# One Wg product per quad of graphs in the second pass, the attention mask added on TensorE, and the first quad's low parts moved to VectorE

## The reference, cut to what matters

```python
h = relu(layernorm(x))
# layer 0
D = abs(h[:, :, None, :] - h[:, None, :, :])      # 64 x 128 x 128 x 128
s = einsum('bijc,oc->bijo', D, W1) + b1           # 64 outputs
s = leaky(batchnorm(s, over=(b, i, j)))
s = einsum('bijo,uo->biju', s, W2)[..., 0] + b2
s = where(adj > 0, s, -9e15)
A = softmax(s, axis=-1)
y = einsum('bij,bjc->bic', A, h) @ Wg.T + bg
y = leaky(batchnorm(y, over=(b, i)))
x = x + concatenate([h, y], 2) @ Wt.T + bt
# layer 1: an attention of the usual kind with a mask, softmax over axis 1, elu, and x added
```

## Time and profile before

| | before |
|---|---|
| median of 3 runs | 1128.88 us |
| their range | 1128.56 to 1129.87 us |
| the profiled execution | 1126.25 us |
| its span | 1124.3 us |
| busy: PE, DVE, ACT, POOL | 1049.5, 1033.1, 1001.0, 567.6 us |
| PE matmul with W1 (line 789) | 1792, 422.8 us |
| PE `att_sum` (lines 931 and 932) | 128 + 128, 24.9 + 24.7 us |
| PE nodes with Wg (line 877) | 128, 18.8 us |

### The profile page before, as it was taken

How to read it: one execution, slowest core, us unless ns; L and a number is a source line. 1 busy time by engine, 2 the same in 40 slices (tenths; PEclk the granted TensorE clock), 3 DMA queues, 4 the chain that set the end, 5 groups by cost and what they waited for, 6 DMA issues and landing times.

```text
span 1124.3 us, 17526 instructions
## 1 busy us (share of the span) xinstructions
PE 1049.5 (93%) x6390; PEld 461.6 (41%) x6390; DVE 1033.1 (92%) x1381; ACT 1001.0 (89%) x1268; POOL 567.6 (50%) x331
## 2 busy tenths in 40 slices
PE   3899999999999899999999989999999999978997
PEld 1333333333333333333333444233333333357786
DVE  5899999999999999999999985899999999948897
ACT  3889898999999899999999978999999999934897
POOL 5687678778777877777787700111121122201430
PEclk9999999999999999999999999999999999989999
DMA  6345443454444344454444487999999999960012
GB/s 183 139 153 196 159 175 153 168 198 168 194 171 179 140 186 180 168 196 169 185 182 178 179 327 269 337 361 329 334 347 326 342 332 329 324 175 14 20 58 76
DMA packets 99060, 233.31 MB, mean 208 GB/s; under 512 B 9120, under 2 KB 46464, under 8 KB 98976
## 3 DMA queue, kind: packets, MB, share of 16 engines
q1 hardware_dynamic: 86704, 219.97, 53.5%
q0 software_dynamic: 2240, 7.34, 1.8%
q10 hardware_dynamic: 10032, 4.89, 1.7%
HBM read 124.43 MB, written 107.74 MB: 206 GB/s over the span
## 4 chain that ended last, share of the span: by engine, by line
PE 50%; DVE 23%; ACT 14%; issue 9%; POOL 3%; ACTq 1%; DMA 0%; DVEq 0%; POOLq 0%
PE psum L789 21%; PE psum L799 10%; ACT store L674 8%; DVE store L294 8%; PE psum L803 8%; DVE plain_st L1099 3%; PE psum L902 3%; ACT store L593 2%; POOL store L294 1%; PE psum L779 1%; PE psum L761 1%; DVE store L1131 1%; PE psum L877 1%; ACTq L678 1%; DVE bst L1283 1%
## 5 line engine op out<-in xcount | busy, mean ns | idle before, releaser
L294 POOL TENSOR_TENSOR store<-h_ext 128x2048 f32<-128x2048 f32 (+1 forms) x96 | 386.3, 4025 | 95.7 <-PE psum L789 95.7
L789 PE MATMUL psum<-store,w1tt_sb 128*64 128x512 f32 x1792 | 422.8, 598 | 10.9 <-ACT store L593 10.8
L294 DVE TENSOR_TENSOR store<-psum,h_ext 128x2048 f32<-128x2048 f32 x160 | 363.9, 2274 | 0.6 <-ACT h_ext L563 0.6
L593 ACT ACTIVATE store<-store 128x2048 f32<-128x2048 f32 x160 | 305.7, 1928 | 19.3 <-DVE store L294 11.8
L674 ACT ACTIVATE store<-store,st 128x1024 f32<-128x1024 f32 x192 | 227.9, 1240 | 0.0
L789 PEld LDWEIGHTS psum<-store,w1tt_sb 128*64 128x64 f32 x1792 | 122.6, 136 | 249.5 <-issue 214.4
L799 PE MATMUL psum<-store,w_twice 128*64 128x512 f32 x768 | 201.6, 602 | 5.4 <-DVE store L294 2.9
L294 DVE TENSOR_TENSOR store<-h_ext 128x2048 f32<-128x2048 f32 x64 | 146.1, 2283 | 16.3 <-PE psum L789 16.0
L1099 DVE BATCH_NORM_STATS2 plain_st<-store 128x6 f32<-128x512 f32 x256 | 160.5, 678 | 0.0
L803 PE MATMUL psum<-early 128*64 128x512 bf16 x1152 | 159.0, 382 | 0.0
L605 ACT COPY store<-psum 128x1024 f32<-128x1024 f32 x128 | 128.4, 1024 | 16.7 <-PE psum L789 11.6
(11 more groups left out here) (161 smaller groups left out, 1088.4 us busy)
## 6 DMA issues: line engine op xcount, KB each, us to landing
kept_products<-store SPq DMA_DIRECT2D x192, 512.0 KB, 2.9
store<-kept_products SPq DMA_DIRECT2D x192, 512.0 KB, 5.8
early<-score_skew POOLq DMA_DIRECT2D x14, 384.0 KB, 6.8
early<-adj SPq DMA_DIRECT2D x16, 256.0 KB, 3.5
early<-adj_t SPq DMA_DIRECT2D x16, 256.0 KB, 3.6
store<-x ACTq DMA_DIRECT2D x16, 256.0 KB, 5.3
out<-early SPq DMA_DIRECT2D x16, 256.0 KB, 2.3
score_skew<-early POOLq DMA_DIRECT2D x14, 128.0 KB, 6.1
```

The costliest lines, as they stand in the source:

```text
L294: return engine.tensor_tensor(t[:, :, 0:steps, :], nodes.unsqueeze(2).broadcast_to([C, 2, steps, N]), windows(h_ext[:, 2 * c, :], STEP * m ...
L593: nc.scalar.activation(t, t, ACT.Abs).then_inc(abs_ready, 1)
L789: last = nc.tensor.matmul(t[MID * g:MID * g + MID, b, :], w1tt_sb[:, 0:MID], diff[slot][:, g, b * BANK:b * BANK + BANK], start=True, stop= ...
```

## The change

1. `mix_at` takes a step: PE makes one quad's product with Wg at n = 14 + 16·k, ACT copies it at n = 17 + 16·k, for k = 0 to 13. All these use bank 4; `at_zero` now waits only for as many as were made before, `at_one` only for the two early ones.
2. `att_sum`: the mask comes first, as one bfloat16 matmul of 512 columns (`neg_ident`, -9e15 on the diagonal, times `none`, 1 where there is no edge); then four float32 matmuls give the transposed half. The plain half is added by DVE when it reads the bank (`att_scores`).
3. POOL makes `neg_ident` once and `none` for each quad (two buffers), ahead of `store_skew(j)`.
4. `s_half` is now read by DVE too, so the next load of it waits for `s_masked` in place of `s_sum`.
5. The first quad's low part is made by DVE at n = 1, not by POOL ahead of its loop.

```diff
+        none = sb("none", [128, 2, BANK], BF16)
+        neg_ident = sb("neg_ident", [128, 128], BF16)
...
         EARLY_MIX = 2
+        WEIGHED, WEIGHED_OUT = 14, 17
 
         def nodes_bank(u):
-            return psum[:, 4 + u % 2, :].rearrange("p (b n) -> p b n", b=QUAD)
-
-        def mix_at(n):
-            u, r = divmod(2 * n, 3)
-            return EARLY_MIX + u if r < 2 and 0 <= u < NQ - EARLY_MIX else None
+            return psum[:, 4 + (u == 1), :].rearrange("p (b n) -> p b n", b=QUAD)
+
+        def mix_at(n, step):
+            u, r = divmod(n - step, QCH)
+            return EARLY_MIX + u if r == 0 and 0 <= u < NQ - EARLY_MIX else None
+
+        def weighed_before(n):
+            return min(EARLY_MIX + so_far(WEIGHED, n), NQ)
...
-            low(0)
             for n in range(CHUNKS):
...
             def load_half(j):
                 pool.wait_ge(skew_stored[j % 2], 16 * (j // 2 + 1))
                 if j > 0:
-                    pool.wait_ge(s_sum, j)
+                    pool.wait_ge(s_masked, j)
...
+            def none_of(j):
+                if j >= 2:
+                    pool.wait_ge(s_sum, j - 1)
+                nc.gpsimd.tensor_scalar(none[:, j % 2, :].rearrange("p (b n) -> p b n", b=QUAD), no_edge[0][:, quad(j), :],
+                                        1.0, None, ALU.mult).then_inc(none_set, 1)
...
+            nc.gpsimd.tensor_scalar(neg_ident[:, :], ident[:, :], NEG, None, ALU.mult).then_inc(neg_set, 1)
             for j in range(NQ):
+                none_of(j)
                 if j < BY_POOL:
                     store_skew(j)
                     load_half(j)
...
-                if u < 2:
+                if u < EARLY_MIX:
                     pe.wait_ge(kept_ready, NKEPT)
                 else:
-                    pe.wait_ge(weighted_ready, u - 1)
+                    at_zero(QCH * (u - EARLY_MIX) + WEIGHED)
...
             def at_zero(n):
 
-                pe.wait_ge(weighted_ready, NQ)
+                pe.wait_ge(weighted_ready, weighed_before(n))
...
             def att_sum(j):
                 pe.wait_ge(half_summed, j + 1)
+                pe.wait_ge(none_set, j + 1)
+                if j == 0:
+                    pe.wait_ge(neg_set, 1)
                 at_zero(QCH * j + SUM)
-                for b in range(QUAD):
-                    nc.tensor.matmul(att[0][:, b, :], ident[:, :], s_half[:, b, 0:N], start=True, stop=False)
-                    last = nc.tensor.matmul(att[0][:, b, :], s_half[:, b, 0:N], ident[:, :], start=False, stop=True)
+                nc.tensor.matmul(att[0], neg_ident[:, :], none[:, j % 2, :], start=True, stop=False)
+                for b in range(QUAD):
+                    last = nc.tensor.matmul(att[0][:, b, :], s_half[:, b, 0:N], ident[:, :], start=False, stop=(b == QUAD - 1))
                 last.then_inc(s_sum, 1)
...
+                if n == 1:
+                    dve.wait_ge(y_mid, 1)
+                    nc.vector.tensor_tensor(y_part(0, 2), by_couple(y_rest[:, :]), y_part(0, 1), ALU.subtract).then_inc(y_split, 1)
...
-                nc.vector.scalar_tensor_tensor(s_shift[:, :, :], no_edge[0][:, quad(j), :], NEG, att[0], ALU.mult, ALU.add)\
+                nc.vector.tensor_tensor(s_shift[:, :, :], att[0], s_half[:, :, 0:N], ALU.add)\
                   .then_inc(s_masked, 1)
```

More of the change, by code:

```diff
@@ L216, in two_layers @@
         x_out, x_folded = sem("x_out"), sem("x_folded")
+        none_set, neg_set = sem("none_set"), sem("neg_set")
         weighted, weighted_ready, y_out = sem("weighted"), sem("weighted_ready"), sem("y_out")
@@ L698, in _ @@
                         load_x(q)
-                if mix_at(n) is not None:
-                    nodes_out(mix_at(n))
+                if mix_at(n, WEIGHED_OUT) is not None:
+                    nodes_out(mix_at(n, WEIGHED_OUT))
                 for step, do in ((Y, y_to_nodes), (EXP, exps)):
@@ L952, in _ @@
                     products_again(n + LEAD_PROD)
-                if mix_at(n) is not None:
-                    weighted_nodes(mix_at(n))
+                if mix_at(n, WEIGHED) is not None:
+                    weighted_nodes(mix_at(n, WEIGHED))
                 m = n - LAG_SCORE
```

4 lines of the change are left out of this document (2 added, 2 removed).

## The result

| | before | after |
|---|---|---|
| median (range) of 4 runs each | 1129.08 us (1128.56 to 1129.87) | 1119.90 us (1118.75 to 1121.02) |
| profiled execution, its span | 1126.25, 1124.3 us | 1118.91, 1116.9 us |
| busy: PE, DVE, ACT, POOL | 1049.5, 1033.1, 1001.0, 567.6 us | 1041.3, 1040.9, 1000.1, 609.1 us |

The account below looks back on a forecast made before the run. PE bounds pass 2's start, a DVE-ACT ring its rounds (20.32 us each). Terms -11.0 + 5.5 - 1.4 - 1.0 = -7.9 take the profiled 1126.25 to 1118.3, or 1121.0 us for the median; range 1114 to 1126.

Parts of the forecast that it names:

- Products out of the start: Start of pass 2: without the products with Wg, ACT runs at 1.12 us a chunk, gaining 11.0 us (bounds 8 to 11.7).
- the 0.7 taken off for PE's clock: Start of pass 2: gain cut from 11.7 to 11.0 us, as PE may stay at 1.2 GHz longer.
- The copy in the ring: Pass 2 rounds: ACT's copy between exponential and result costs 0.46 us in twelve rounds, 5.5 lost (bounds 0 to 11).
- the ring: Pass 2 rounds: DVE waits for ACT (0.43 us) and ACT for DVE (1.16), closing 20.32 us a round without PE.
- rival A: Pass 2 rounds: the chain through PE's scores and `att_sum` binds; 1.4 us gained instead of 5.5 lost, 1114.1; chance 0.12.
- `att_sum`, -1.4 at the end: Quads 14 and 15: PE's `att_sum` is 0.7 us shorter each, gaining 1.4 us (bounds 0 and 1.4); nothing in the rounds.
- The sum on DVE and the added waits: Pass 2: DVE's sum replaces the mask there at 0.68 us; waits for `none_set`, bank 4 and `s_masked` are covered; 0.
- POOL's masks: Pass 2 rounds: 16 masks of some 1.51 us on mostly idle POOL don't hold up DVE; cost 0.
- rival C: Pass 2 rounds: POOL's masks block DVE in the ring, costing 23 us, 1144; chance 0.08.
- Start of pass 1: PE begins 1.2 us later, but its 2.54 us wait for ACT goes; gain 1.0 (bounds: loss 1.3, gain 1.4).
- The caution about PE's slow pace: Start of pass 1: gain taken as 1.0 us, not 1.3, since PE's slow first us may last as long by the clock.

Follow-up runs that it names:

- Spread alone: Kernel before with only the products with Wg moved to one per quad (n = 14 + 16k, ACT's copy at n = 17 + 16k): median 1122.9 us, ratio 0.9956.
- copy outside: Changed kernel with products with Wg at n = 10 + 16k and ACT's copy at n = 12 + 16k, ahead of the exponential: median 1118.7 us, ratio 0.9912.
- all together: Changed kernel with ACT's copy ahead of the exponential, POOL's masks moved, loads of x on SP, products of no use on PE: 1118.8 us, ratio 0.9905.

## Why the prediction was right

It gave 1121.0 us, in a range of 1114 to 1126; 1119.9 came. By its own steps:

1. *Products out of the start, -11.0: -9.4.* ACT's rate held but for 0.01 (1.13 us a chunk for 1.12, some 0.4 in all), and the loads kept up (DMA at 1.01 to 1.10). Mis-sized was the 0.7 taken off for PE's clock and the wait before the exponential: the new waits for L805 are 1.27 us, and 0.83 stands before exponential 0 in place of the 0.21 that was carried over. With PE kept at 2.4 GHz the start came to 54.05 and 53.56.
2. *The copy in the ring, +5.5: +5.7 of the +6.94.* Spread alone, 20.80; copy outside, 20.32. The choice of the ring over the chain's reading (rival A, 1114.1) was the step that mattered most, and it rests on two waits, 0.43 and 1.16. The prediction has both "in every round"; ACT's is, but DVE's is missing in three rounds of before (at 779.64, 921.92 and 942.25), of which under 6. After the change the chain of waits itself shows the ring.
3. *`att_sum`, -1.4 at the end: about right.* It takes 1.20 us (895.89 to 897.09), DVE's wait for it in quad 15 (0.89 in the earlier trace rows) is gone, and ACT's wait before each of the two last exponentials falls from 4.37 or 4.38 to 3.62: 1.5 us in all. The other 1.5 us of the -3.02 was not foreseen. ACT's issues of the loads of x start when PE's last product made again is done, 0.70 behind the start of exponential 13 before (989.08) and 0.04 after (984.02); its last activation comes 1.16 sooner behind that exponential, and the second eight issues take 5.34 in place of 5.68. Of those sixteen issues the prediction said nothing, though they cost the changed kernel some 6 us (medians 1119.9 and 1113.8) and stood in the trace of before.
4. and 5. *The sum on DVE and the added waits, 0.* L1247 takes 0.68; no wait for bank 4, `none_set` or `s_masked` shows in the rounds.
6. *POOL's masks, 0: +1.2 us.* This step failed, in the direction of rival C and at a twentieth of its price. The row it rested on, a subtraction of 2.27 beside a mask of 1.51, was read as no contention; it shows no more than that this DVE instruction went free. Others didn't: in the changed kernel L1150 takes 1.52 to 1.79 in place of 1.23 where it meets POOL, L298 up to 2.80 in place of 2.27, and the masks of layer 0 that DVE holds up 2.46 to 4.23 in place of 1.49. The trace of before had a warning that the prediction didn't show:

```profile
919.60 1.64 DVE L1131 TENSOR_SCALAR store<-store 128x2048 int32<-128x2048 int32 x1
...
920.25 2.35 POOL L526 TENSOR_SCALAR early<-no_edge 128x512 f32<-128x512 uint8 x1
```

It comes three times there (at 777.33, beside POOL's sum of the half, at 919.60 and at 939.93), 0.41 or 0.42 each, and DVE's wait of 0.43 for ACT, which is gone in just these rounds, took it in. That the eight rounds with L526 were no longer than the four without it was this cover, and not a lack of contention.

The Trainium skill's rule (SBUF — State Buffer, "Who interferes with whom": the instruction that is second to issue blocks until the first is done) comes near POOL's side of it. Held to the end of DVE's subtraction at 897.93, a mask of 1.49 would end at 899.42; it ended at 899.94. It fits the small DVE instruction of 128x4 elements at 19.69, done when POOL was. It doesn't fit DVE's large ones: none lost a whole mask; they lost up to 0.56 in the changed kernel (1.79 for 1.23) and 0.85 in the kernel with all together (3.12 for 2.27).

7. *Start of pass 1, -1.0: -1.93.* PE's first product came at 22.43, forecast 22.4, and the wait for ACT went as described. The caution about PE's slow pace was too great: PE's first products at full pace start at 26.79, and at 27.15 before, 0.36 earlier by the clock and not later; the two chunks took 6.9 us in place of the 7.9 that the prediction carried over, and the gain was kept.

That the sum was off by only 0.5 is luck, since errors cancel: the start of pass 2 gave 1.6 less and the rounds cost 1.4 more than forecast, the end gave 1.6 more and the start of pass 1 0.9 more. The last two lay outside the bounds that the prediction had put on them, and the masks had been given none.

## What to carry to other kernels

Where several engines are all nine tenths full, look in a round for two waits that name each other. They close a ring, an instruction inside it costs its full length in every round, and the same instruction outside it costs nothing until the next bound, here DVE, which lay 0.43 us away. Look at more than one round: a wait that is missing in some of them tells what else is near its limit. A DMA issue is an instruction of its engine too: eight of them cost 5.4 us ahead of a ready activation, and moved to a free queue they have to stand behind, not ahead of, the small store that the chain needs next.

## What the runs showed of the hardware

- PE's granted clock fell to 0.50 behind an idle time of 2.69 us in five profiled executions and not in six others with the same idle time; the fall cost 1.5 to 1.6 us. It stayed at 1.00 in both executions with eight short products in the idle time. Between the passes it fell to 0.50 or 0.52 in ten of eleven executions; with eight products of 0.9 us each it stayed at 1.00 (but they delayed the real ones), and so it did with four, without delay.
- An instruction of POOL that reads one-byte data from SBUF (128x512) took up to 4.23 us in place of 1.49 beside two DVE instructions in a row. Where it met POOL, DVE's subtraction took 2.27 to 2.80 in the changed kernel (3.12 in one with the masks moved), and its in-place integer operation 1.52 to 1.79 in place of 1.23.
- One issue of a load of 256 KB kept its sequencer 0.37 to 0.53 us for the first four or more in a row, and 0.51 to 1.92 for the later ones, with the data of the first on its way: 12.93 and 13.35 us for sixteen.
